# A linear layer inside a graph network: GpSimd adds the scaled own rows, TensorE adds the bias in PSUM

## The reference, cut to what matters

```python
x = x + _L1_gnn_ref(_layernorm(x, axis=-1), edge_index, L1_gnn_W, L1_gnn_a_left, L1_gnn_a_right)
x = x + _L1_ffn_ref(_layernorm(x, axis=-1)[None], L1_ffn_weight, L1_ffn_bias)[0]
x = x + _L2_gnn_ref(_layernorm(x, axis=-1), edge_index, L2_gnn_W, L2_gnn_b, L2_gnn_bn_w, L2_gnn_bn_b)
```

## Time and profile before

| What | Value |
|---|---|
| Time, median of 3 runs | 7910.3 us (7909.39 to 7918.43) |
| Profiled execution, its own time | 7921.19 us |
| Span of its instructions | 7919.4 us |
| DVE busy, whole span | 3609.7 us (46%) |
| POOL busy | 4682.5 us (59%) |
| PE busy | 5157.7 us (65%) |
| ACT busy | 3195.4 us (40%) |
| First and last work of the stage | 2080 us to 2238.5 us of the span |

### The profile page before, as it was taken

How to read it: one execution, slowest core, us unless ns; L and a number is a source line. 1 busy time by engine, 2 the same in 40 slices (tenths; PEclk the granted TensorE clock), 3 DMA queues, 4 the chain that set the end, 5 groups by cost and what they waited for, 6 DMA issues and landing times. The chain is left out here.

```text
span 7919.4 us, 115948 instructions
## 1 busy us (share of the span) xinstructions
PE 5157.7 (65%) x22196; PEld 4061.3 (51%) x22197; DVE 3609.7 (46%) x8810; ACT 3195.4 (40%) x8284; POOL 4682.5 (59%) x4875
## 2 busy tenths in 40 slices
PE   2689867777645555779734344566677566676796
PEld 2566544454434444579734344345456345455795
DVE  7634467777820000453500000466666566667533
ACT  2533244444343433333333333244444344444432
POOL 5032277777567777125277777677774777773253
PEclk9779977777777777779755555577778777777698
DMA  2432144444233333222311111344443344442324
GB/s 61 176 78 83 48 120 117 115 117 116 83 100 108 109 109 108 66 78 70 100 28 28 28 28 26 91 115 115 115 114 83 103 115 115 114 114 66 106 69 137
DMA packets 417887, 726.44 MB, mean 92 GB/s; under 512 B 129365, under 2 KB 278315, under 8 KB 414167
## 3 DMA queue, kind: packets, MB, share of 16 engines
q0 software_dynamic: 208256, 503.58, 23.6%
q1 hardware_dynamic: 202475, 208.74, 8.5%
q10 hardware_dynamic: 6508, 8.01, 0.3%
HBM read 596.63 MB, written 123.54 MB: 91 GB/s over the span
## 5 line engine op out<-in xcount | busy, mean ns | idle before, releaser
L1017 POOL DMA_INDIRECT g_rows<-table,src_idx x2326 | 2218.0, 954 | 710.0 <-issue 709.4
L1292 PE MATMUL g_p_win<-g_rows,g_hot 128*128 128x264 f32 (+1 forms) x4704 | 1502.2, 477 | 44.5 <-issue 41.4
L1292 PEld LDWEIGHTS g_p_win<-g_rows,g_hot 128*128 128x128 f32 x4704 | 1069.1, 238 | 305.3 <-issue 94.0
L1182 ACT ACTIVATE g_hot<-iota,near 128x128 f32<-128x128 f32 x2352 | 720.7, 386 | 411.7 <-PE g_p_win L1292 375.7
L1017 POOL DMA_INDIRECT g2p_rows<-rows,src_idx x771 | 736.3, 955 | 235.2 <-issue 235.2
L1017 POOL DMA_INDIRECT gcnp_rows<-table,src_idx x771 | 734.8, 953 | 235.5 <-issue 235.5
L1098 DVE TENSOR_TENSOR g_rows<-g_rows,g_p_w 128x1792 f32<-128x1792 f32 x336 | 679.0, 2021 | 27.0 <-ACT g_rows L1210 2.7
L1201 ACT ACTIVATE g_resets_f<-fwd_reset 128x112 f32 (+3 forms) x168 | 54.8, 326 | 1176.1 <-DVE g_b L1069 1061.3
L1249 PE MATMUL g_p_turn<-slide,g_a 128*8 128x128 f32 (+1 forms) x168 | 59.0, 351 | 715.6 <-DVE g_a L1057 715.6
L1105 DVE TENSOR_TENSOR agg<-agg,g2p_p_out 128x256 f32 x112 | 42.1, 417 | 943.3 <-PE g2p_p_out L1254 943.3
L1105 DVE TENSOR_TENSOR agg<-agg,gcnp_p_out 128x64 f32 x112 | 20.3, 221 | 957.0 <-PE gcnp_p_out L1254 957.0
(11 more groups left out here) (831 smaller groups left out, 10986.2 us busy)
## 6 DMA issues: line engine op xcount, KB each, us to landing
g_stage<-table SPq DMA_DIRECT2D x3328, 1.0 KB
g_rows<-table,src_idx POOLq DMA_INDIRECT x2326
g2p_stage<-rows SPq DMA_DIRECT2D x1664, 1.0 KB
gcnp_stage<-table SPq DMA_DIRECT2D x1664, 0.2 KB
back<-agg SPq DMA_DIRECT2D x7, 1792.0 KB, 34.9
rows<-r_row SPq DMA_DIRECT2D x98, 128.0 KB, 3.0
gcn_row_in<-back SPq DMA_DIRECT2D x14, 896.0 KB, 7.3
c_row<-back SPq DMA_DIRECT2D x14, 896.0 KB, 13.5
```

The costliest lines, as they stand in the source:

```text
L1017: gp.indirect_dma_start(rows[:, s, j, 0:width + H], None, table, bass.IndirectOffsetOnAxis(g.src_idx[:, at:at + 1], 0)).then_inc(got[s], 16)
L1182: last = nc.scalar.activation(hot[:, j, :], g.iota[:, :], ACT.Square, scale=-1.0, bias=g.near[:, bass.ds(c * J + j, 1)])
L1292: last = nc.tensor.matmul(p_win[:, 0:W], hot[:, j, :], rows[:, s, j, :], start=(j == 0), stop=(j == J - 1))
```

## The change

VectorE's `mix` goes. GpSimd, behind each `own_share(n)`, adds the scaled own rows of the group to x (1792 elements on each of 128 partitions), and signals `own_added` by that; VectorE's `add(n)` now waits for `scaled` and for this, and adds the scaled sums alone. GpSimd's order becomes own_share(0), add of 0, own_share(1), add of 1 and so on, with no wait for ScalarE. The 49 bias adds of GpSimd go, and with them VectorE's wait for `biased`. The bias is loaded as one row of one partition, and TensorE, ahead of each tile's product, multiplies a row of ones by it into the same PSUM tile (49 matmuls of 1 row and 256 columns).

```diff
--- before.py
+++ after.py
@@ -606,7 +606,7 @@
                 behind(i)
         ahead_of_all(NT, normalise, copy)
 
-    def tensor(self, pe, rhs):
+    def tensor(self, pe, rhs, bias=None):
         nc = self.nc
 
         def turn(i, s):
@@ -621,8 +621,10 @@
             pe.wait_ge(self.copied, i + 1)
             if i >= 2:
                 pe.wait_ge(self.taken, i - 1)
+            if bias is not None:
+                nc.tensor.matmul(self.out[s][:, :], self.g.ones[0:1, :], bias, start=True, stop=False)
             for b in range(2):
-                last = nc.tensor.matmul(self.out[s][:, :], self.xt[:, s, b, :], rhs[:, b, :], start=(b == 0), stop=(b == 1))
+                last = nc.tensor.matmul(self.out[s][:, :], self.xt[:, s, b, :], rhs[:, b, :], start=(b == 0 and bias is None), stop=(b == 1))
             last.then_inc(self.multiplied, 1)
         ahead_of_all(NT, turn, multiply)
 
@@ -1340,13 +1342,13 @@
     with Phase(nc, name) as ph:
         own = ph.sb("own", [P, 2, GROUP, D])
         total, inv, share = (ph.sb(n, [P, NT, H]) for n in ("total", "inv", "share"))
-        w_in, wt, bias_wide = ph.sb("w_in", [P, 2, D]), ph.sb("wt", [P, 2, D]), ph.sb("bias_wide", [P, D])
+        w_in, wt, bias_row = ph.sb("w_in", [P, 2, D]), ph.sb("wt", [P, 2, D]), ph.sb("bias_row", [1, D])
         p_w = ph.ps("p_w", [P, 4, P])
         first, second = GroupNorms(nc, g, ph, "a"), GroupNorms(nc, g, ph, "b")
         prod = FedProducts(nc, g, ph, D, first)
         seq, w_loaded, bias_loaded, turned, placed = (ph.sem(n) for n in ("seq", "w_loaded", "bias_loaded", "w_turned", "w_placed"))
-        shared, own_scaled, own_added, scaled, added, biased, made, stored = (
-            ph.sem(n) for n in ("shared", "own_scaled", "own_added", "scaled", "added", "biased", "made", "stored"))
+        shared, own_scaled, own_added, scaled, added, made, stored = (
+            ph.sem(n) for n in ("shared", "own_scaled", "own_added", "scaled", "added", "made", "stored"))
         loaded = [ph.sem(f"loaded{s}") for s in range(2)]
         heads_of = lambda t: t.rearrange("p a (h c) -> p a h c", h=H)
         wide = lambda t: t.unsqueeze(3).to_broadcast([P, GROUP, H, C])
@@ -1358,7 +1360,7 @@
                     sp.dma_start(own[:, n % 2, :, :], table[n * GROUP * P:(n + 1) * GROUP * P, 0:D].rearrange("(t p) d -> p t d", p=P)).then_inc(loaded[n % 2], 16)
                 load(0)
                 sp.dma_start(w_in[:, :, :], w.rearrange("(b p) n -> p b n", p=P)).then_inc(w_loaded, 16)
-                sp.dma_start(bias_wide[:, :], bias.rearrange("(o n) -> o n", o=1).to_broadcast([P, D])).then_inc(bias_loaded, 16)
+                sp.dma_start(bias_row[:, :], bias.rearrange("(o n) -> o n", o=1)).then_inc(bias_loaded, 16)
                 load(1)
                 for n in range(NG):
                     if n + 2 < NG:
@@ -1379,16 +1381,11 @@
                     o = own[:, n % 2, :, :]
                     gp.wait_ge(loaded[n % 2], 16 * (n // 2 + 1))
                     G.tensor_tensor(heads_of(o), heads_of(o), wide(share[:, of(n), :]), ALU.mult).then_inc(own_scaled, 1)
+                    gp.wait_ge(own_scaled, n + 1)
+                    G.tensor_tensor(g.x[:, of(n), :], g.x[:, of(n), :], o, ALU.add).then_inc(own_added, 1)
                 gp.wait_ge(shared, 1)
-                own_share(0)
-                own_share(1)
-                gp.wait_ge(bias_loaded, 16)
                 for n in range(NG):
-                    if n + 2 < NG:
-                        own_share(n + 2)
-                    for t in range(n * GROUP, (n + 1) * GROUP):
-                        gp.wait_ge(prod.normal, t + 1)
-                        G.tensor_tensor(g.x[:, t, :], g.x[:, t, :], bias_wide[:, :], ALU.add).then_inc(biased, 1)
+                    own_share(n)
 
             @block.vector
             def _(dv):
@@ -1408,14 +1405,9 @@
                     sums = g.agg[:, of(n), 0:D]
                     V.tensor_tensor(heads_of(sums), heads_of(sums), wide(inv[:, of(n), :]), ALU.mult).then_inc(scaled, 1)
 
-                def mix(n):
-                    sums = g.agg[:, of(n), 0:D]
-                    dv.wait_ge(scaled, n + 1)
-                    dv.wait_ge(own_scaled, n + 1)
-                    V.tensor_tensor(sums, sums, own[:, n % 2, :, :], ALU.add).then_inc(own_added, 1)
-
                 def add(n):
                     x = g.x[:, of(n), :]
+                    dv.wait_ge(scaled, n + 1)
                     dv.wait_ge(own_added, n + 1)
                     V.tensor_tensor(x, x, g.agg[:, of(n), 0:D], ALU.add).then_inc(added, 1)
                     dv.wait_ge(added, n + 1)
@@ -1423,7 +1415,6 @@
                 def take(t):
                     x = g.x[:, t, :]
                     dv.wait_ge(prod.multiplied, t + 1)
-                    dv.wait_ge(biased, t + 1)
                     V.tensor_tensor(x, x, prod.out[t % 2][:, :], ALU.add).then_inc(prod.taken, 1)
                     if t >= 1:
                         again(t - 1)
@@ -1447,8 +1438,6 @@
                         if n + 1 < NG:
                             if u == 0 and n >= 0:
                                 scale(n + 1)
-                            if u == 1:
-                                mix(n + 1)
                             if u == 2:
                                 add(n + 1)
                             if u >= 3:
@@ -1491,7 +1480,8 @@
                     for ib in range(2):
                         nc.tensor.transpose(p_w[:, 2 * ob + ib, :], w_in[:, ob, ib * P:(ib + 1) * P], g.ident[:, :]).then_inc(turned, 1)
                 pe.wait_ge(placed, 4)
-                prod.tensor(pe, wt)
+                pe.wait_ge(bias_loaded, 16)
+                prod.tensor(pe, wt, bias_row[0:1, :])
 
 
 def tile_of(t, i, n):
```

## The result

The changed kernel takes 7985.14 us (median of 6 runs, 7980.94 to 7990.6) against 7912.55 us before (6 runs, 7909.39 to 7918.43): **+72.6 us**. The ratio is 1.0093, with a 95% interval of 1.0083 to 1.0104. Forecast were 7908.9 us and a range from 7891 to 7925; the time is outside it, on the slow side. The profiled execution has a span of 7987.6 us (7919.4 before).

What follows compares the result with a forecast made beforehand. VectorE was taken to bound the stage (91% busy in its middle). -14.1 + 10.5 - 1.1 + 3.3 = -1.4 us, from a median of 7910.3 to 7908.9 us; range 7891 to 7925.

Steps and rivals of the forecast that it cites:

- the price of the bias on TensorE: 49 bias matmuls on TensorE: hidden in the middle at high clock; tail +1.3, half-clock tiles +2, together +3.3 us, between 0 and +12.
- Rival 3: TensorE becomes the bound at half clock, 2.98 us a tile: +25 us, 7935 us; chance 0.05.
- The signal that was named: Granted TensorE clock of the middle: the prediction is wrong if it falls below 0.75.
- `mix` goes, -14.1 us: VectorE's own work: seven `mix` operations of 2.02 us, all on the path, disappear, -14.1 us.
- What GpSimd's instructions block, +10.5 us: VectorE blocked by GpSimd's 14 long instructions, 2.05 us each: 28.7 against 18.2 us before, +10.5; between -4.2 and +26.7.
- rival 2: In `spread` and `fit`, each GpSimd instruction blocks VectorE for its whole length: +14.8, 7925 us; slower from 2.15 each; chance 0.13.
- the first `fit`: Lead-in on VectorE: 2 to 4 us later than 2104.7 if own_share(1) gets in ahead of add(0).
- The price of GpSimd's add, 3.21 us: A 1792-wide add on GpSimd, taken as long as `own_share`, 3.21 us; the skill's figure would give 3.9.
- Loads, stores and the wait for `biased`: Loads hold GpSimd up 2 us at most, VectorE not at all; no store gets later; VectorE's wait for `biased` goes, -1.1 us.

## Why the prediction was wrong

**The step that failed** is the price of the bias on TensorE: "the bias is hidden", 3.3 us, between 0 and 12. It was priced from full-weight products of the same columns, as if the number of rows did not matter. With 128 rows it would have held: 1.5 us a tile was measured, and the product costs 6.0 us in the profile (118.8 against 112.8) and 3.6 in the medians. With one row the term is 61.3 + 6.0 = 67.3 us, over five times the upper bound. Two effects make it: the clock, and the stops of 0.6 us a tile.

**Rival 3** was the mechanism, with a chance of 0.05 and a price of +25 us. It spoke of a clock that stays low, and weighed the clock by the work of TensorE ("gets more work and fewer gaps"); that a busy TensorE can be kept low by what it runs was not considered. Its tile of 2.98 us, measured so with 128 rows, became 3.58 by the stops: 49 x 0.60 = 29.4 us more. 49 x 3.58 = 175.4 us, and with the begin and the last takes the 180.1 of the profile. The signal that was named, a clock of the middle below 0.75, is there: 0.50. The Trainium skill has the rule for the stops (TensorEngine Tiling (Array Packing), section Tiling Modes): changing the tiling mode drains TensorE, and its modes differ by 128, 64 or 32 rows. It was not weighed. The page does not say that a plain product of one row is such a change; the trace agrees that it is one: 0.65 us ahead of each load of 128 rows behind a product of one row, and at low clock 3.58 us a tile with 64 rows as with one. What in the one-row product holds the clock down stays open, as said above.

**`mix` goes, -14.1 us:** right in kind; without mix and with nothing in its place, the kernel is 17.0 us faster, 14.4 of it in the tiles of the two profiles. A group beside which GpSimd does nothing takes 14.2 us, and near 14 was forecast.

**What GpSimd's instructions block, +10.5 us:** too low, and its place was wrong. VectorE's blocked time in the changed kernel is 6.6 us in L1412 (20.7 - 7 x 2.02), 5.8 in L1406 (20.0 less the same) and 3.8, 3.5, 3.1, 2.9 and 1.2 in L472, L484, L470, L473 and L468, together 26.9 us for 14 instructions, 1.9 each where 2.05 was taken:

```profile
L1412 DVE TENSOR_TENSOR x<-x,agg 128x1792 f32<-128x1792 f32 x7 | 20.7, 2963 | 3.3 <-POOL x L1385 3.1
...
L1406 DVE TENSOR_TENSOR agg<-agg,l_inv 128x1792 f32<-128x1792 f32 x7 | 20.0, 2851 | 0.2
...
L472 DVE SCALAR_TENSOR_TENSOR l_a_gap<-l_a_gap 128x7 f32<-128x7 f32 x7 | 4.9, 696 | 0.0
L484 DVE SCALAR_TENSOR_TENSOR shift<-l_a_mean,rstd 128x7 f32<-128x7 f32 x7 | 4.7, 671 | 0.4 <-DVE rstd L483 0.2
L470 DVE TENSOR_TENSOR l_a_var<-l_a_stats 128x7 f32<-128x7 f32 x7 | 4.2, 595 | 0.0
L473 DVE SCALAR_TENSOR_TENSOR l_a_var<-l_a_var,l_a_gap 128x7 f32<-128x7 f32 x7 | 4.1, 590 | 0.2
```

19.8 us of it fall before the first tile (7.9 in the kernel before), as rival 2 described it: a queued GpSimd instruction slips into the gaps of `spread` and `fit`. With the wait of 3.1 us for GpSimd's first add, which the prediction took to be in the 14, and 2.0 us less of `mix`, that is 11.9 + 3.1 - 2.0 = 13.0 us, and the lead-in is 12.8 us longer; the first `fit` had been put at 2 to 4 us later. The fair test of the term is the change without the bias product, in which TensorE hides none of the late groups: the same rows there, with 3.7 us in the seven L471 and 3.6 in the seven L468 of the second statistics, make 33.6 us, 2.4 for each of the 14, and rival 2's bound for slower was 2.15. So the term was 33.6 - 18.2 + 3.1 = 18.5 us, and -14.1 + 18.5 - 1.1 = +3.3 with 1.6 more of waits for products (12.4 against 10.8) is 4.9, against 4.4 measured in that profile and 8.0 in the medians. The terms had given -14.1 + 10.5 - 1.1 = -4.7.

**The price of GpSimd's add, 3.21 us:** too low. The free ones take 3.95 us:

```profile
L1383 POOL TENSOR_TENSOR l_own<-l_own,l_share x7: 3199/3208/3217, 2081.7 to 2210.2; 128x1792 f32<-128x1792 f32 x7
L1385 POOL TENSOR_TENSOR x<-x,l_own x7: 3953/5625/5837, 2085.0 to 2213.5; 128x1792 f32<-128x1792 f32 x7
```

The Trainium skill's figure (GPSIMD Engine Reference, section 3.1) had given an estimate of 3.9 us, and the prediction set it aside. It agrees with this. `own_share`, whose second input is a broadcast of one value over 32 elements, stays at 3.21.

**Loads, stores and the wait for `biased`:** no transfer of the tiles is waited for by any other engine than GpSimd, as forecast. But the loads were to hold GpSimd up by 2 us at most, and it was to be idle after 2145 to 2150. In SP's order, which the prediction read for the stores alone, the loads of groups 5 and 6 stand behind the stores of groups 0 and 1; GpSimd waits 62.4 and 16.0 us for them in the changed kernel and starts its last add at 2213.5.

## What to carry to other kernels

A product of few rows is not priced by its columns. Between products of 128 rows it stops TensorE twice and can hold its clock down, so fill the rows with zeros if they are not needed (61 us here), and look at the granted clock beside the busy share before calling an engine's spare time free. Work moved from VectorE to GpSimd is still VectorE's time where both read two inputs from SBUF; a long GpSimd instruction ahead of a chain of short VectorE steps costs its full length, and it must be kept out of the lead-in by a wait (21.4 against 37.3 us to the first tile) or left where it was, and even so it can cost more than it saves (12.5 us with five of the seven adds moved). A load that stands in a DMA queue behind a store begins when the store's rows are done, however early its buffer is free.

## What the runs showed of the hardware that had not been expected

- TensorE stays at a granted clock of 0.50 for 170 us at 98% busy, when each tile has one product of one row beside six records of 128 rows; with 128 rows in its place it is at 0.90, with 64 rows in between (0.50 to 1.00 by stretches). A one-row product of 64 columns is enough for 0.50.
- Changing between 128 rows and 64 or 1, there and back, costs 0.6 us a tile at the low clock, the same for 64 rows and for one, and 0.4 us at the high clock, which 64 rows alone show.
- GpSimd's add of two full inputs, 128x1792, takes 3.95 us, its product of the same size with a second input that is one value over 32 elements 3.21 us, while a 128x256 add takes 0.72 us. Whether the input or the operation makes the difference was not tried.
- A VectorE step with one input (L471, seven elements, 0.17 us when free) took 3.84 us beside GpSimd's add once, in the kernel without the bias product.
